# First attention: the scaled q made by ScalarE and GpSimd instead of VectorE

## The reference

```
qk = x @ Wqk + bqk ; v = x @ Wv + bv ; n = x @ Wn + bn
scores = q . k                    (16 heads of 8 numbers)
attn = scores * causal_mask / exp(n)
out = (attn @ v) @ Wo + bo
```

## Time and profile before

| what | value |
|---|---|
| median of 3 runs | 1408.18 us (1398.48 to 1413.44) |
| profiled execution, its own time | 1396.88 us |
| its span, first to last instruction | 1395.1 us |
| first attention in it | about 20 to 340 us |
| mean granted TensorE clock | 0.936 of full speed |
| busy share of TensorE, VectorE, ScalarE, GpSimd | 89%, 75%, 54%, 60% |

### The profile page before, as it was taken

One profiled execution on the slowest core, in us unless ns is written; L12 is line 12 of the kernel. 1 busy time (PEld: TensorE's weight loads), 2 busy tenths in 40 slices (PEclk: granted clock), 3 DMA queues, 4 the chain that ended last, 5 costly groups with the idle time before them and its releaser, 6 DMA issues.

```text
span 1395.1 us, 28372 instructions
## 1 busy us (share of the span) xinstructions
PE 1239.1 (89%) x8534; PEld 787.4 (56%) x8534; DVE 1042.0 (75%) x4462; ACT 756.4 (54%) x1901; POOL 836.4 (60%) x1246
## 2 busy tenths in 40 slices
PE   3999998996999999999999999999999999999100
PEld 1566665565898965454545445545455469888100
DVE  2899999895674458898999989989998856565322
ACT  2444444442665767666676756656676546556000
POOL 3237776777525224356777767766874445367776
PEclk9999999997999998998999989999999899999655
DMA  6845602011556520000100001011000125466522
GB/s 174 259 154 192 197 30 87 28 44 60 171 163 210 166 65 16 14 11 24 32 25 29 32 24 32 29 62 48 29 28 14 44 79 162 150 218 205 150 75 75
DMA packets 119783, 125.80 MB, mean 90 GB/s; under 512 B 15568, under 2 KB 109904, under 8 KB 119632
## 3 DMA queue, kind: packets, MB, share of 16 engines
q1 hardware_dynamic: 103248, 90.42, 20.5%
q0 software_dynamic: 16384, 33.59, 7.9%
HBM read 50.15 MB, written 73.79 MB: 89 GB/s over the span
## 4 chain that ended last, share of the span: by engine, by line
PE 70%; DVE 12%; POOL 7%; issue 4%; DMA 2%; ACT 2%; SPq 0%; POOLq 0%; ACTq 0%; DVEq 0%
PE pair L1897 25%; PE pair L1823 8%; POOL vmyg L564 6%; PE pair L1685 5%; DVE pT L1401 5%; PE bank L1709 4%; PE pair L1834 4%; PE pair L1812 2%; PE bank L1630 2%; PE bank L1624 2%; PE pair L1674 2%; DVE xs L1318 2%; PE bank L1936 1%; PE bank L1916 1%; PE pair L1695 1%
## 5 line engine op out<-in xcount | busy, mean ns | idle before, releaser
L1897 PE MATMUL pair<-kT,apart 32*128 32x512 f32 x2048 | 460.2, 672 | 3.5 <-DVE smax L1401 2.0
L1401 DVE CUSTOM_DVE_ANT_0 pT<-pair,pT 128x256 f32<-128x256 f32 x1024 | 384.2, 416 | 76.1 <-ACT pT L925 70.4
L925 ACT ACTIVATE pT<-pair 128x256 f32<-128x256 f32 x1024 | 327.0, 397 | 196.8 <-PE pair L1897 193.3
L1897 PEld LDWEIGHTS pair<-kT,apart 32*128 32x128 f32 x2048 | 192.8, 192 | 128.1 <-DVE smax L1401 78.7
L564 POOL DMA_INDIRECT vmyg<-ybufA,slg x128 | 123.7, 966 | 110.6 <-DVE smax L1401 67.9
L1823 PE MATMUL pair<-xeT,unit_w 128*128 128x256 f32 x768 | 184.6, 384 | 0.0
L564 POOL DMA_INDIRECT vmyg<-ybufB,slg x128 | 122.8, 959 | 71.3 <-DVE smax L1401 33.6
L509 POOL DMA_INDIRECT dispB<-xnf,sli x128 | 129.3, 1010 | 57.0 <-issue 35.2
L509 POOL DMA_INDIRECT dispA<-xnf,sli x128 | 130.0, 1016 | 50.9 <-issue 30.2
L1128 DVE TENSOR_TENSOR pT<-pair,causal 128x1024 f32<-128x1024 f32 x128 | 151.2, 1213 | 12.1 <-PE pair L1685 11.2
L1293 DVE TENSOR_TENSOR hid<-sg,pair 128x512 f32<-128x512 f32 x96 | 65.7, 685 | 123.3 <-ACT sg L851 123.1
(11 more groups left out here) (231 smaller groups left out, 1947.6 us busy)
## 6 DMA issues: line engine op xcount, KB each, us to landing
dispB<-zeros SPq DMA_DIRECT2D x16, 1408.0 KB
apart<-dispA SPq DMA_DIRECT2D x96, 128.0 KB
ybufA<-ye SPq DMA_DIRECT2D x48, 256.0 KB
apart<-dispB SPq DMA_DIRECT2D x96, 128.0 KB
ybufB<-ye SPq DMA_DIRECT2D x48, 256.0 KB
dispA<-zeros SPq DMA_DIRECT2D x33, 128.0 KB
xs<-in_x SPq DMA_DIRECT2D x16, 256.0 KB, 3.1
out<-xs SPq DMA_DIRECT2D x15, 256.0 KB, 2.6
```

Of the source, the lines that this page charges most:

```text
L925: act.activation(rel[n % RING][:, q, :], pair[n % RING][:, q, HALF:SEQ], ACT.Relu).then_inc(s["relu_done"], 1)
L1401: dve.tensor_tensor_reduce(out=rel[n % RING][:, q, :], in0=pair[n % RING][:, q, 0:HALF], in1=rel[n % RING][:, q, :], scale=1.0, scalar=LOW ...
L1897: pe.matmul(pair[n % RING][:, q, :], apart[h][at, j, t * P:(t + 1) * P], kTs[h][at, HALF:], start=True, stop=True).then_inc(s["bsc_done"], 1)
```

## The change

For batches 1 to 15 `scaled_q` leaves VectorE's stream. In its place ScalarE copies q with its bias from PSUM into the qT tile (`biased_q`), ahead of its copy of k. GpSimd multiplies the tile by `einv` in place. GpSimd does this after its wait for the residual sum and ahead of `send_rest(3, 12)` and `norm_scale(b + 2)`. Batch 0 keeps VectorE's instruction. There is one new semaphore, `qb_ready`, from ScalarE to GpSimd.

```diff
@@ gpsimd, attention_a
                 if b >= 4:
 
                     pool.wait_ge(s["x1_ready"], b)
+                if next:
+                    pool.wait_ge(s["einv_ready"], b + 2)
+                    pool.wait_ge(s["qb_ready"], b + 1)
+                    pool.tensor_tensor(qTs[1 - h][:, :], qTs[1 - h][:, :], einv[:, :], ALU.mult).then_inc(s["qT_ready"], 1)
                 send_rest(3, 12)
                 norm_scale(b + 2, norm_width(b))
@@ scalar
+            def biased_q(b, h):
+
+                act.wait_ge(s["q_done"], b + 1)
+                act.activation(qTs[h][:, :], bank[0][:, :], ACT.Identity, bias=cols[:, 0:1]).then_inc(s["qb_ready"], 1)
+
             def keys_turns(b, h):
 
+                if b:
+                    biased_q(b, h)
                 act.wait_ge(s["k_done"], b + 1)
@@ vector, attention_a
-                if next:
-                    scaled_q(b + 1, 1 - h)
                 row_aggregates(call, W)
```

More of the change, by code:

```diff
@@ L239, in build @@
                  "slg_ready got0 got1 got_end comb_head combined_head comb0 combined "
-                 "n_done q_done k_done kv_done einv_ready qT_ready turns_ready kT_ready lefts past_done stats2 unit_w_act tok_ready vm_ready pv_done sc_done pT_ready state_done stm_ready ctxT_ready o_done "
+                 "n_done q_done qb_ready k_done kv_done einv_ready qT_ready turns_ready kT_ready lefts past_done stats2 unit_w_act tok_ready vm_ready pv_done sc_done pT_ready state_done stm_ready ctxT_ready o_done "
                  "bproj_done qm_ready bkT_ready selrow_done xsel_done att_scaled ffn_scaled xselq_ready xctx_done xctx_ready bsc_done relu_done bmax_done kdiff_done vbias_done vout_done voutb_done mT_done mTs_done m8_done m8i_done m8f_done idg_done "
```

## The result

The changed kernel takes 1439.63 us (median of 4 runs, 1434.97 to 1444.32), the kernel before 1404.55 (4 runs, 1398.48 to 1413.44). The ratio is 1.0245, with a 95% interval of 1.0175 to 1.0314: **slower by 35 us**, inside the range that was forecast (1416 to 1456) and 2.6 us above its 1437. That it is slower is clear; whether by more than 2% the interval leaves open.

A forecast was written before the change was run, and what follows sets the result against it. The prediction took TensorE to bound the first attention, VectorE following closely. Waits of 27 us plus 7 for the clock made +34 us, on a base of 1403: 1437 us, with an 8 in 10 range of 1416 to 1456.

The forecast's parts named there:

- VectorE's gain of nothing: First attention: removing 15 products, 11.3 us of VectorE's work, gains nothing, since TensorE's gapless work covers it.
- The price of the multiplication: Each of GpSimd's 15 added 128x512 multiplications takes 1.30 us, as its `add_bias` does.
- ScalarE's delays: Late k copy costs TensorE 0.1 us per body, late masked copies 0.15 at first scores; counted only in bodies 0 to 3.
- The place in GpSimd's queue: Multiplication starts 0.09 us behind ScalarE's copy, ahead of two DMAs and the norm, making everything behind 2.68 us late.
- The loop: First attention: q's projection through the norm and TensorE's turn to the next q takes 20.92 us per body, against 18.32.
- a delay paid once: Rival: GpSimd's idle time takes up the lateness, so it does not repeat per body; about 1408 us, chance 0.07.
- Two of the signs named: Profile after: TensorE waits over 2 us per body at the turns; VectorE has 2 to 3 us more idle time.
- The waits: First attention: nine bodies at 2.6 us, 1.0 for bodies 0 to 3, 2.7 at the end; sum +27 us.
- The last delay: GpSimd's lateness from body 14 passes through body 15 to the end of the stage whole: 2.7 us.
- The clock: TensorE's clock falls in the new waits: nine waits x 0.5 x 1.7 us = 7.7, ends 0 and 15.
- The sum: Waits 27 plus clock 7 make +34 us, put on the base of 1403: 1437 us.

The follow-up runs named there:

- e1: Changed kernel without the product by the inverse scale on any engine for batches 1 to 15, ScalarE's copy of q kept: 1409.11 us, ratio 1.004.
- e4: Changed kernel with GpSimd's multiplication moved behind the two DMAs of send_rest(3, 12), still ahead of the norm: 1413.39 us, ratio 1.0071.
- e6: Changed kernel with one dummy matmul on TensorE ahead of each of the two turns in bodies 5 to 15: 1426.30 us, ratio 1.0175.
- e5: The changed kernel run again, unaltered, as a reference and for a second profile: 1439.48 us, ratio 1.0237.
- e7: Changed kernel with a second 128x512 multiplication, of constants, on GpSimd right behind the first: 1482.11 us, ratio 1.0544.
- e2: Changed kernel with VectorE, not GpSimd, multiplying q in place after ScalarE's copy: 1411.11 us, ratio 1.0056.

## Why the prediction was right

**VectorE's gain of nothing** was right: e1 takes the product away and the body is not shorter.

**The price of the multiplication**, 1.30 us from `add_bias`, measured 1.27.

**ScalarE's delays.** The 0.1 us through the late copy of k appears alone in e1, 0.13 per body. In the changed kernel TensorE's first scores wait in one of the bodies 5 to 14 only (0.39 us, shown above).

**The place in GpSimd's queue** was the step that carried the forecast, and it held: the norm is 3.05 us later behind q than before in the body shown and about 2.75 in the others, where the sum had 2.68. The difference is the start of the multiplication behind ScalarE's copy: 0.47 us in the body shown (209.13 + 0.69 to 210.29), 0.17 in the ten others (233.56 + 0.69 to 234.43, for one), not 0.09. Moving two DMAs past it brings back over half of the lengthening (e4).

**The loop.** 20.92 us were forecast, 20.98 and 21.28 measured at full clock. That it is a loop, and not a delay paid once, shows in every body of the first table. Two of the signs named came out beside their bounds: the turns wait 1.94 us per body, not over 2, and VectorE's added idle time reaches 3.3 us, not 3.

**The terms of the stage.** The waits came out right in sum, though not in their parts. In e6, where the clock stays up to the end of body 14, the stage ends 24.8 us later than before. The kernel before has a fall of the clock in body 11, worth 1.7 us, which e6 does not have; so the waits make about 26.5 us, against 27 forecast. Between the turns of bodies 4 and 15 they make 25.4, where the sum had 23.4. The last delay, 2.7 us through body 15, nearly vanished. Before, GpSimd's weight copies there began with gaps of 1.18 us and three of 0.3, put down to issue; in the changed kernel they follow one another. The first pair before, and all eight after:

```profile
315.98 1.03 POOL L587 COPY unit_w<-f_w 128x384 f32 x2 [1.18 <-issue]
```

```profile
360.28 3.70 POOL L587 COPY unit_w<-f_w 128x384 f32 x8
```

From the end of q's projection to the second turn of `xnf` in body 15 it is 28.6 us (349.9 to 378.5), against 28.1 before: 0.5 instead of 2.7. Why the gaps are gone was not tried.

**The clock** is the term that was mis-sized: 7.7 us, with an end at 15; about 18 in the profile after. Each body that fell, against one at full clock of its kind: 2.9 + 4.5 + 2.9 + 1.5 from the table, and against the same bodies of e6 26.33 - 23.21 = 3.1 for body 10 and 23.49 - 20.63 = 2.9 for body 14. The sum took a half of nine bodies, and six fell; but one fall costs 3.0 us on average rather than 1.7, since most of them last longer than the one in the earlier trace rows. Against before 1.7 go off, for the fall of body 11 that the changed kernel does not have. The profile after is the slowest of its four runs; by the medians of e5 and e6 the clock is worth 13 us, inside the ends of the term.

**The sum.** Waits and clock together give 42 us in the profiled pair, as the stage shows, against 34 forecast (the terms as written add up to 34.8, not 34). The medians differ by 35. The profile of before is 8 us below its median, and that of after 5 above; the remaining 5 us of the spans lie in the second attention, which the change does not touch: 670.0 us in the profile before, 677.6 after, and 673.9 to 684.0 in the eight experiments. One execution per side says less than the medians. That the forecast came within 3 us of the median is in part luck: the clock term was too small, by some 5 us by the medians and 8 to 10 by the profiles, and the last delay was 2.2 too large. The mechanism and the wait per body are not luck; they were read in advance and show in the trace.

## What to carry to other kernels

Before moving work to an engine with idle time, read what stands behind the new instruction in that engine's queue, and who waits for it with how much in hand: here the 0.22 us in hand of the layernorm decided, not GpSimd's 4 us of idle time. If the new instruction waits for something late, put independent work of its queue ahead of it, and close the loop to see whether the delay repeats. When TensorE at full clock is given a short wait in each round, price the clock as well as the wait.

## What the runs showed of the hardware that was not expected

- Length of waits and falls of TensorE's clock to its lower level (1.2 GHz), in bodies of 19 to 27 us: one wait of 1.09 us per body (e4), none to 335 us; two, of 1.12 and 0.82 (after, e5), a fall in six and in five of ten bodies; one of 2.1 to 2.8 and one of 0.4 to 0.8 (e7), in all of them. Two dummy matmuls in these waits kept the clock up (e6).
- GpSimd started its multiplication 0.17 us behind ScalarE's copy in most bodies, but 0.47 in one of the changed kernel and 0.48 in one of e6, which is the body of 21.28 us instead of 20.98. It is the same body, b = 8, in these two and in e5, so it is not chance from run to run; in e7 it is not there. What decides it was not found.
- A GpSimd multiplication of 128x512 took 1.27 us with two different inputs and the result in place of one of them, 1.04 with one tensor as both inputs and the result in another tile. Which of the two differences counts was not tried.
- GpSimd's indirect DMA beside VectorE's product of two SBUF tiles (e2) took 1.48 us in all eleven bodies. Between 110 and 330 us, none took over 1.15 in the nine other traces.
